# Attention part of a fused block: the square of the centred sum moves behind the last gelu on ScalarE, a value copy moves ahead of the third gelu, and two low parts change places on GpSimd

## The reference, cut to what matters

```python
xn = layernorm(xt) ; xs = roll(xn, (-3, -3))            # windows of 7 x 7 = 49 tokens
q, k, v = split(xw @ qkv_w + qkv_b)                     # 3 heads of 16
attn = softmax(q k^T * 16**-0.5 + bias)                 # per window and head
x  = x + roll_back((attn v) @ proj_w + proj_b)          # first residual ("x1")
xn = layernorm(x)                                       # centre, square, variance
h  = gelu(xn @ fc1_w + fc1_b)                           # 48 -> 192
x  = x + h @ fc2_w + fc2_b                              # second residual ("x2")
```

## Time and profile before

| | |
|---|---|
| median of 3 runs | 1960.83 us (1960.3, 1960.83, 1974.0) |
| profiled execution | 1975.34 us |
| its span in the profile | 1973.7 us |
| PE busy | 1772.9 us (90%) |
| ACT busy | 1541.7 us (78%) |
| DVE busy | 1365.0 us (69%) |
| POOL busy | 1170.0 us (59%) |
| mean granted PE clock | 0.951 |

### The profile page before, as it was taken

The page is one execution under the profiler, slowest core; times in us unless marked ns, Lnnn a source line. Parts: engine busy times, 40 slices in busy tenths (PEclk is TensorE's granted clock), DMA queues, the critical chain, the costliest instruction groups (busy, mean ns, idle before and its releaser), DMA issues. The chain is left out here.

```text
span 1973.7 us, 90330 instructions
## 1 busy us (share of the span) xinstructions
PE 1772.9 (90%) x38186; PEld 1076.4 (55%) x38186; DVE 1365.0 (69%) x2016; ACT 1541.7 (78%) x2904; POOL 1170.0 (59%) x1048
## 2 busy tenths in 40 slices
PE   4999999999999999999999998995899967999996
PEld 2666556656565565655666565651497943333332
DVE  7776666767676676766767676642777766888883
ACT  3788788888888788888888888873766647888882
POOL 5687686777778677777877777652255550122222
PEclk9999999999999899999999999996799985999998
DMA  4344554444444344444444444411488759999994
GB/s 111 94 108 99 139 129 103 105 102 110 100 113 102 96 107 100 116 99 105 106 107 103 104 112 99 98 45 43 109 216 216 214 135 170 227 253 253 262 258 147
DMA packets 233228, 262.26 MB, mean 133 GB/s; under 512 B 167079, under 2 KB 179911, under 8 KB 232711
## 3 DMA queue, kind: packets, MB, share of 16 engines
q1 hardware_dynamic: 217478, 217.50, 46.2%
q0 software_dynamic: 15360, 39.08, 6.6%
HBM read 160.82 MB, written 80.88 MB: 122 GB/s over the span
## 5 line engine op out<-in xcount | busy, mean ns | idle before, releaser
L416 POOL TENSOR_TENSOR shift<-const_b,qmax 113x588 bf16<-113x588 bf16 x256 | 299.4, 1170 | 231.8 <-DVE qmax L511 230.1
L563 DVE TENSOR_TENSOR x<-ps_m,x 112x392 f32<-112x392 f32 x128 | 66.5, 561 | 272.8 <-PE ps_m L1028 272.8
L511 DVE TENSOR_REDUCE qmax<-ps_s 113x12 f32<-113x588 f32 x256 | 194.9, 761 | 66.8 <-PE ps_s L907 66.7
L1487 POOL DMA_DIRECT2D out_rolled<-r_OUT x128 | 63.8, 503 | 270.2 <-DVE r_OUT L1587 270.2
L716 ACT ACTIVATE P<-ps_t 113x588 f32<-113x588 f32 x256 | 172.0, 672 | 58.4 <-PE ps_t L959 57.1
L748 ACT ACTIVATE G<-ps_m 128x392 f32<-128x392 f32 x384 | 178.3, 500 | 46.0 <-PE ps_m L1009 45.5
L503 DVE TENSOR_TENSOR Ul<-Uf 113x784 bf16<-113x784 f32 x192 | 208.5, 1113 | 0.0
L1333 PE MATMUL conv_ps<-xin,band_now 64*64 64x448 bf16 x2688 | 203.1, 364 | 2.2 <-DVE x_low L1228 2.2
L406 POOL TENSOR_TENSOR xhl<-xh 113x784 bf16<-113x784 f32 x64 | 200.7, 3137 | 2.2 <-DVE xh L551 2.2
L709 ACT COPY Uf<-ps_m 113x392 f32<-113x392 f32 x384 | 172.9, 486 | 33.0 <-PE ps_m L874 24.8
L1333 PE MATMUL conv_ps<-x_low,band_now 64*64 64x448 bf16 x1344 | 179.6, 351 | 0.0
(11 more groups left out here) (244 smaller groups left out, 5203.9 us busy)
## 6 DMA issues: line engine op xcount, KB each, us to landing
xin<-rows_scratch SPq DMA_DIRECT2D x96, 236.0 KB, 3.8
XT<-x_tokens SPq DMA_DIRECT2D x64, 294.0 KB, 3.3
X<-x_windows SPq DMA_DIRECT2D x128, 147.0 KB, 3.4
RS<-rs_scratch SPq DMA_DIRECT2D x128, 147.0 KB, 3.4
XR<-x_windows SPq DMA_DIRECT2D x128, 147.0 KB, 3.2
x_scratch<-x SPq DMA_DIRECT2D x128, 147.0 KB, 3.4
y_scratch<-y POOLq DMA_DIRECT2D x96, 196.0 KB, 2.9
r_RS<-rs_scratch SPq DMA_DIRECT2D x128, 147.0 KB, 4.6
```

The costliest lines, as they stand in the source:

```text
L416: nc.gpsimd.tensor_tensor(shift[:, j % 2], e, m, ALU.mult).then_inc(S["md"], 1)
L511: nc.vector.tensor_reduce(qmax[:, j % 2, :].rearrange("p (b n) -> p b n", b=2), ps_s[0:R, :, 0:2 * HQ].rearrange("p b (n t) -> p b n t", t ...
```

## The change

Two lists of calls are reordered; no instruction is added, removed or changed in size. On ACT, `square(prv)` goes from behind the first gelu to behind the sixth, and `keep_values(s, 3)` from behind the third gelu to ahead of it. On POOL, `low0(nx2)` goes ahead of `squares_low(prv)`.

```diff
@@ attention_phase, gpsimd, step
                 centre_tokens(s.at(4))
                 make_shift(nxt, 0)
+                low0(nx2)
                 squares_low(prv)
-                low0(nx2)
@@ attention_phase, scalar, step
                     nc.scalar.preload_act_table_set("gelu_and_others")
                 gelu(old, 0, 0)
-                square(prv)
                 gelu(old, 0, 1)
+                keep_values(s, 3)
                 gelu(old, 1, 0)
-                keep_values(s, 3)
                 gelu(old, 1, 1)
                 gelu(old, 2, 0)
                 gelu(old, 2, 1)
+                square(prv)
                 if old.real:
                     nc.scalar.preload_act_table_set("natural_log_exp_and_others")
                 exp_scores(s, 3)
```

## The result

The changed kernel takes **2000.55 us** (median of 4 runs, 1997.42 to 2005.08) against 1962.38 for the kernel before in the same comparison (4 runs, 1960.3 to 1974.0): **ratio 1.0186, 95% interval 1.0147 to 1.0225, slower**. The forecast was 1990 with a range of 1973 to 2010 and slower by over 1%. The profiled execution took 2005.08 us, 29.7 more than the profiled one of before.

The account below looks back on a forecast made before the run. Bound: a PE block of some 14 us plus a 6.15 us gelu stretch where ACT and PE release one another. 56 x 0.53 - 5 x 0.19 = +28.7 us on 1960.8 gives 1989.5, say 1990 us; range 1973 to 2010.

Parts of the forecast that it names:

- The chain of the gelu stretch: ACT: square behind gelu 6 delays table load and exponential, so PE starts the next keys_and_values at 729.12 instead of 728.59.
- 0.53 a step: Start of the next step's keys_and_values on PE: 0.53 us later in each undisturbed step, bounds 0.38 to 0.63.
- The waits that were to show it: ACT idle 0.27 ahead of gelu 3 and 0.66 ahead of gelu 5; PE 0.72 ahead of keys_and_values, ended by the exponential.
- Nothing is given back: PE block after the stall has 0.05 us idle; ACT still waits 0.56 for PE, so the delay stays.
- POOL's order costs nothing: Swapped low parts on POOL: later shift of group 1 stays hidden, variance keeps 2.1 us of slack; no cost.
- SP's swap transfers go 1.45 us earlier: nothing: SP's queue behind low0: transfers leave 1.45 us earlier into a buffer read a step or more later; no effect.
- Which steps pay, and the sum: Of 61 steps, 56 lose 0.53 us and five with a fallen clock gain 0.19; sum +28.7 us.
- (1): Rival: ACT's order doesn't bind, only fc2 starts earlier; 11.6 us faster, 1949 us; chance 5%.
- (2): Rival: PE's clock falls more often, 20 more falls at 2.5 us, +50 on top, 2040 us; chance 7%.
- (3): Rival: delay real but smaller, or the five clock falls vanish; +8, 1969 us, within 1%; chance 13%.

Follow-up runs that it names:

- experiment 1: Kernel before with only the square moved behind the last gelu, copy and low parts unmoved; 1994.16 us, ratio 1.0127.
- experiment 4: Changed kernel with the square placed between gelu 4 and gelu 5; 1969.2 us, ratio 1.0009 to the kernel before.
- experiment 7: Changed kernel with the square made twice, the second behind the first; 2058.68 us, ratio 1.0466 to the kernel before.
- experiment 3: Kernel before with only the two low parts on POOL swapped; 1969.74 us, ratio 1.0012.
- experiment 8: Changed kernel with the low parts on POOL back in the old order; 1990.79 us, ratio 1.0123 to the kernel before.
- experiment 9: Changed kernel timed again, nothing altered; 2007.95 us, ratio 1.0194 to the kernel before.
- experiment 10: Changed kernel with the low parts on POOL in the old order, timed again; 1993.65 us, ratio 1.0127 to the kernel before.
- experiment 6: Changed kernel with the square behind the exponential of group 3, last on ACT; 1993.41 us, ratio 1.0127 to the kernel before.
- experiment 11: Changed kernel with SP's swap transfers also waiting for the shift of group 1; 1996.79 us, ratio 1.0143 to the kernel before.
- Experiment 2: Changed kernel with the square back behind gelu 1, copy and low parts still moved; 2004.92 us, ratio 1.0171 to the kernel before.
- experiment 5: Changed kernel with the square made on VectorE behind a step's last maximum instead of on ACT; 1957.07 us, ratio 0.995 to the kernel before.
- experiment 12: Changed kernel with the square on VectorE and the low parts on POOL in the old order; 1983.74 us, ratio 1.0084 to the kernel before.

## Why the prediction was right, and where it wasn't

- **The chain of the gelu stretch: right, to some hundredths.** Predicted in the old time: gelu 5 at 725.29, square 726.07, table load 727.02, exponential 728.31, PE 729.12. Measured, 31.67 taken off: 725.29, 726.06, 727.03, 728.32 and 729.08. Experiments 1, 4 and 7 hold it up from three sides: the square alone makes it, in a gap it costs nothing, and doubled it adds 0.97.
- **0.53 a step: 0.51** (20.60 against 20.09). PE started 0.10 behind the exponential's end, not 0.15. The waits that were to show it are shorter in the profile than forecast: 0.17 and 0.54 of ACT for 0.27 and 0.66, 0.50 of PE for 0.72. The starts agree to 0.04 at most; the profile counts a wait from the end of the instruction before, which lies later than the time at which the engine could have taken the next. And PE's wait has "issue" for its releaser where the exponential's name was forecast.
- **Nothing is given back: right.** All undisturbed steps of the changed kernel are 20.6; ACT still waits 0.52 for PE ahead of the next exponential (0.56 predicted).
- **POOL's order costs nothing: right for the step** (experiments 3 and 8), with more room than was said: the maximum of group 2 doesn't wait for the shift of group 1, though the prediction had it so (experiment 8). The moved low part of the square took 1.49, as forecast with VectorE waiting beside it.
- **"SP's swap transfers go 1.45 us earlier: nothing": the step that failed.** Their reader has indeed a step and more, but the transfers themselves are not neutral: with the late square, the new order against the old costs 0.67% of 1968, 13 us (experiments 9 and 10), in irregular steps. In the kernel before, the same swap cost nothing that can be told (experiment 3), and experiment 6 has it for nothing too. With SP held back 11 of 14 us are gone (experiment 11), so the cost comes through the time of the transfers; why only in this kernel stays open. The prediction looked only at who waits for them.
- **Which steps pay, and the sum.** The prediction let the five steps with a fallen clock go free (28.7 instead of 31 us). The changed kernel's profile has two such steps, of 23.61 and 21.52 us; before they were 23.66 and 23.76 at the longest and 21.52 at the shortest, so such a step did not grow. The sum as measured has three parts. The chain is 61 x 0.51 = 31. With the low parts in the old order (experiments 1, 8 and 10) the whole is only 24 to 25 us by the ratios, so 6 to 7 us went elsewhere: their profiles have less in irregular steps than before's, and one to three steps with a fallen clock where before's has five. But before's profile is of an execution 13 us above its median, with a mean clock as low as in any run of that kernel (0.951, against up to 0.960), so that falls went away in a usual execution is not shown. The transfers are 13. Together 37 to 38, measured 36.5 (1.0186) and 38 (1.0194). The forecast's 28.7 lacked the last term and the one before it; that they partly cancel is luck. The range held because its upper end allowed for more falls and for the spread of before's runs, not because it had the transfers.
- **The rivals.** (1), that the order doesn't bind, fell: PE stood still where it was said to. (2), more falls of the clock, fell for this kernel: two steps in place of five, though the new stall of 0.5 is there in every step. The Trainium skill's warning (TensorE: Matmul & The Clock Gate, A second HAM failure mode: psum-queue depth-cycling) speaks of brief idling between groups; in these runs the falls go with stalls close together. Experiment 2, with 0.51 and 0.90 in the gelu stretch, has eight steps with falls. In the kernel before, four of the five come in steps in which PE stood for another 0.43 to 1.28 us just ahead of that stretch, and so does the longer one of the changed kernel (0.95). A single stall of 0.5 behind fc2, or of 0.63 at `variance` (experiment 6, no falls), did not bring them; one of 1.48 behind fc2 did in three steps of experiment 7, each time behind that stall. These are counts from one profile each. (3), that falls go away, may be true in part, as said above; the time did not end within 1%.

## What to carry to other kernels

In a hand-ordered schedule look for the place where an engine waits anyway: work there is free, and the same work behind the last wait, ahead of a table load and an activation that the next step needs, costs all of itself once the slack there is used up (0.51 of the square's 0.94 here, 0.97 for the second square of experiment 7). An operation that "only moves" also moves the DMAs behind it; ask what they pass in time, not only who reads them. And where an engine is full and another stands still for 3.9 us at the same moment, moving the operation over was worth more than any order tried here (experiment 5); but the same move with another order on GpSimd made the kernel slower than before (experiment 12), so look at what the two engines then do side by side.

## What was not expected of the hardware

- The time at which a train of transfers goes out changed this kernel's time by some 11 to 14 us in 2000, although nothing was seen to wait for it: PE stops for 0.2 to 0.8 us (once each 1.3 and 1.9 in experiments 10 and 11), also within runs of small matmuls between which the program has no wait (experiments 9 to 11).
- VectorE's addition of a per-partition value to a 113x784 fp32 tile in SBUF took 1.62 us beside a GpSimd operation that ran until 0.4 us before its end (experiment 5), and 0.62 with GpSimd waiting (experiment 12, below). The product of the same tile with itself took 0.98 in both, and GpSimd stood still beside it in both:

```profile
1138.36 0.62 DVE L550 TENSOR_SCALAR xc<-xc,centred_b 113x784 f32<-113x784 f32 x1
1139.01 0.98 DVE L554 TENSOR_TENSOR sq<-xc 113x784 f32<-113x784 f32 x1
```

- Two low parts on VectorE beside one on GpSimd: 1.85 and 3.31 us when GpSimd is first, 3.25 and 2.22 when VectorE is.
